# GNN layer with an eight-expert feed-forward layer: all experts for every node, in groups of 256, in place of routing

## What is computed

```python
# gnn
msgs = layernorm(x)[src] * edge_weight[:, None]
agg = segment_sum(msgs, dst, 12500)
x = x + agg @ W.T + b
# feed-forward, E = 8 experts, HID = 1024
xf = layernorm(x)
H = gelu(xf @ W1 + b1)                       # 1024 wide
probs = softmax(H @ Wg + bg)                 # 8 wide
assign = argmax(probs)
for e in range(8):
    y = H @ Wd[e] + bd[e]                    # 1024 x 256 each
    out = out + where(assign == e, probs[:, e:e+1] * y, 0)
x = x + out
```

## Time and profile before

| | |
|---|---|
| median of 3 runs | 2819.68 us (2818.2 to 2826.73) |
| span of the profiled execution | 2820.7 us |
| PE busy | 2418.9 us (86%) |
| POOL busy | 1847.0 us (65%) |
| DVE busy | 988.5 us (35%) |
| ACT busy | 444.4 us (16%) |
| granted TensorE clock, mean | 0.953 |

### The profile page before, as it was taken

One profiled execution on the slowest core, in us unless ns is written; L12 is line 12 of the kernel. 1 busy time (PEld: TensorE's weight loads), 2 busy tenths in 40 slices (PEclk: granted clock), 3 DMA queues, 4 the chain that ended last, 5 costly groups with the idle time before them and its releaser, 6 DMA issues.

```text
span 2820.7 us, 40486 instructions
## 1 busy us (share of the span) xinstructions
PE 2418.9 (86%) x11774; PEld 1410.7 (50%) x11775; DVE 988.5 (35%) x2788; ACT 444.4 (16%) x847; POOL 1847.0 (65%) x1988
## 2 busy tenths in 40 slices
PE   0468998998889889899899899898998968999998
PEld 0133444444444444444444444444444447888887
DVE  8421333333333323333233333233332463333332
ACT  7000011000111000110001101011100102443442
POOL 0677777777777777777777777777777103555553
PEclk9988999999999999999999999999999989999999
DMA  9433444444444444444444444444444254555553
GB/s 390 151 111 112 149 146 137 120 140 149 147 149 125 126 149 148 147 141 120 138 145 148 147 118 132 148 150 148 143 121 133 90 177 129 184 183 176 183 184 126
DMA packets 153599, 420.32 MB, mean 149 GB/s; under 512 B 33320, under 2 KB 67499, under 8 KB 150880
## 3 DMA queue, kind: packets, MB, share of 16 engines
q0 software_dynamic: 100032, 300.27, 35.8%
q1 hardware_dynamic: 53536, 119.73, 11.4%
HBM read 328.02 MB, written 92.82 MB: 149 GB/s over the span
## 4 chain that ended last, share of the span: by engine, by line
POOL 46%; PE 31%; issue 17%; DVE 2%; DMA 2%; DVEq 0%; ACT 0%; SPq 0%; POOLq 0%; ACTq 0%
POOL big L391 46%; PE psA L519 4%; PE psH L560 4%; PE psA L641 3%; PE psG L641 3%; PE psH L641 3%; PE psE L641 3%; PE psR L503 2%; PE psE L509 1%; DMA src_i<-in_srcT 1%; PE psA L581 1%; PE psA L538 1%; PE psH L631 1%; PE psE L631 1%; PE psA L631 1%
## 5 line engine op out<-in xcount | busy, mean ns | idle before, releaser
L391 POOL DMA_INDIRECT big<-xn_table,src_i x1664 | 1615.2, 971 | 581.5 <-issue 580.0
L519 PE MATMUL psA<-w,ident 128*128 128x512 f32 x1664 | 735.5, 595 | 0.0
L519 PEld LDWEIGHTS psA<-w,ident 128*128 128x128 f32 x1664 | 308.5, 190 | 347.9 <-issue 347.9
L503 PE MATMUL psR<-big,sel_narrow 128*32 128x256 f32 x3328 | 258.7, 464 | 220.9 <-DMA big<-xn_table,src_i 158.6
L454 ACT ACTIVATE hidT<-psH,b 128x512 f32<-128x512 f32 x200 | 137.4, 687 | 1651.6 <-PE psH L560 1651.6
L560 PE MATMUL psH<-xn2T,w 128*128 128x512 f32 x800 | 351.4, 592 | 0.7 <-ACT xn2T L449 0.7
L503 PEld LDWEIGHTS psR<-big,sel_narrow 128*32 128x32 f32 x3328 | 116.0, 128 | 369.0 <-issue 333.5
L877 DVE COPY parts<-psR 128x512 f32<-128x512 f32 x104 | 71.8, 690 | 563.3 <-PE psR L503 562.9
L560 PEld LDWEIGHTS psH<-xn2T,w 128*128 128x128 f32 x800 | 152.1, 190 | 181.5 <-issue 179.2
L509 PE MATMUL psE<-w,ident 128*128 128x512 f32 x416 | 224.2, 664 | 0.0
L405 POOL COPY stage<-rel_f 128x1 int32 (+1 forms) x105 | 19.2, 183 | 250.9 <-DVEq L1065 144.3
(11 more groups left out here) (203 smaller groups left out, 2343.4 us busy)
## 6 DMA issues: line engine op xcount, KB each, us to landing
row_table<-rows SPq DMA_DIRECT2D x25, 2064.0 KB, 7.9
big<-xn_table,src_i POOLq DMA_INDIRECT x1664
big<-in_x SPq DMA_DIRECT2D x10, 1280.0 KB, 17.4
xn_table<-big SPq DMA_DIRECT2D x10, 1280.0 KB, 12.8
big<-in_x SPq DMA_DIRECT2D x25, 512.0 KB
row_table<-big SPq DMA_DIRECT2D x25, 512.0 KB, 3.9
big<-in_Wd SPq DMA_DIRECT2D x8, 1024.0 KB, 11.9
hidT<-in_dstT SPq DMA_DIRECT2D x2, 840.0 KB, 30.3
```

Of the source, the lines that this page charges most:

```text
L391: nc.gpsimd.indirect_dma_start(out=xring[:, h * STEP_TILES + j, :], out_offset=None, in_=xn_dram[:, :], in_offset=bass.IndirectOffsetOnAxi ...
L503: mm = nc.tensor.matmul(psQ[j * LANES:(j + 1) * LANES, o * C:(o + 1) * C], sel_narrow[:, t, :], xring[:, t, :], start=(odd == 0), stop=(od ...
L519: nc.tensor.matmul(psA[0][:, :], ident[:, :], w1[:, 0, 0:512], start=True, stop=True)
```

## The change

- Groups are 256 nodes (`GROUP = 256`), so 49 in place of 25. Layer-norm chunks at the start are 7 of 14 rows in place of 10 of 10.
- There is no routing stage and no row table. In a node step PE multiplies the hidden layer of each block of 128 nodes with all of Wd, two experts at a time (512 columns): a `unit` is 8 products, and a group has 2 blocks x 4 pairs = 8 units. DVE adds each unit into x with a factor per node and expert, `mask`, which is the probability for the expert of the largest logit and zero for the others (`route`, `add_unit`). The expert's bias comes from a product of the transposed mask with bd (`bias`).
- A group's first block runs in its own node step, its second block in the next group's node step, mixed with that group's messages, transposes and hidden layer (`group`). The last group's second block comes at the end.
- Wd (8 MB) is loaded once, behind the step tables, and stays in SBUF.
- The products of constants (COVER and FILL) are gone. The first edge products and the placing go by octets of tiles, each octet with its own PSUM bank, copy and semaphore count. The narrow one-hots have one buffer in place of three.
- x is held in two halves by turns, loaded ahead, and stored to the output when all units are added. ACT loads its table for Exp and back for GELU in each group.

```diff
 from contextlib import ExitStack
 import concourse.bass as bass
@@ -30,11 +20,13 @@
 E = 8
 EPS = 1e-5
...
+PAIRS = E // 2
 EDGES = 212500
 STEP_TILES = 16
 NG = -(-EDGES // (P * STEP_TILES))
...
-FILL = 8
 TILES = NG * STEP_TILES
 TABLE = TILES + STEP_TILES
 STEPS = NG + NF
-SLOT = GROUP + P
-NS = 1 << (2 + -(-STEP_TILES * P // GROUP) - 1).bit_length()
+FIELDS = 8
...
+            sp.wait_ge(s_tabs, 1)
             for e in range(E):
-                sp.dma_start(wd[:, e * HC:(e + 1) * HC, :],
-                             Wd[e].rearrange("(c p) o -> p c o", p=P)).then_inc(s_wd, 16)
-            sp.dma_start(bd_bc, bd.rearrange("e c -> (e c)").partition_broadcast(P)).then_inc(s_bd, 16)
+                sp.dma_start(wd[:, :, e * C:(e + 1) * C],
+                             Wd[e].rearrange("(k p) o -> p k o", p=P)).then_inc(s_wd, 16)
...
-            def hidden(f):
+                    nc.scalar.activation(xn2T[:, k, :], psH[k][:, 0:GROUP], ACT.Identity).then_inc(s_xtc, 1)
                 for c in range(HC):
                     act.wait_ge(s_h, f * HC + c + 1)
...
                                          bias=b1[:, c:c + 1]).then_inc(s_gelu, 1)
...
-                routed_act(t, t % RING2)
+                nc.scalar.activation(gate_parts[:, :], psG[:, 0:GROUP], ACT.Identity).then_inc(s_gc, 1)
+                act.wait_ge(s_below, f + 1)
+                nc.scalar.activation(expv[:, :, :], below[:, :, :], ACT.Exp).then_inc(s_exp, 1)
+                nc.scalar.preload_act_table(ACT.Gelu)
+                act.wait_ge(s_mt, f + 1)
+                nc.scalar.activation(mask_t[:, :], psG[0:E, 0:GROUP], ACT.Identity).then_inc(s_mtc, 1)
...
-                                t = h * STEP_TILES + o * OCT + 2 * j + odd
-                                mm = nc.tensor.matmul(psQ[j * LANES:(j + 1) * LANES, o * C:(o + 1) * C],
-                                                      sel_narrow[:, t, :], xring[:, t, :],
+                                t = o * OCT + 2 * j + odd
+                                mm = nc.tensor.matmul(bank[o][j * LANES:(j + 1) * LANES, 0:C], sel_narrow[:, t, :],
+                                                      xring[:, h * STEP_TILES + t, :],
                                                       start=(odd == 0), stop=(odd == 1))
-                    mm.then_inc(s_edge_mm, STEP_TILES)
-                    for _ in range(COVER):
-                        nc.tensor.matmul(psW[:, :], ident[:, :], w1[:, 0, 0:512], start=True, stop=True)
-                    pe.wait_ge(s_parts, g + 1)
+                        mm.then_inc(s_edge_mm, OCT)
                     for o in range(OCTS):
+                        pe.wait_ge(s_parts, g * OCTS + o + 1)
                         for k in range(KC):
-                            at = (o * KC + k) * SPAN
-                            mm = nc.tensor.matmul(psW[:, at:at + SPAN], parts[:, o, k * P:(k + 1) * P],
+                            mm = nc.tensor.matmul(bank[o][:, k * SPAN:(k + 1) * SPAN], parts[:, o, k * P:(k + 1) * P],
                                                   place[:, o, :], start=True, stop=True)
-                    mm.then_inc(s_placed, 1)
-                    for _ in range(FILL):
-                        nc.tensor.matmul(psA[0][:, :], ident[:, :], w1[:, 0, 0:512], start=True, stop=True)
...
+            def dense(to, b, pair, k):
+                return nc.tensor.matmul(to[:, :], hidT[:, k, b * P:(b + 1) * P],
+                                        wd[:, k, pair * 2 * C:(pair + 1) * 2 * C], start=(k == 0), stop=(k == HC - 1))
+            def unit(to, b, pair):
+                for k in range(HC):
+                    mm = dense(to, b, pair, k)
+                mm.then_inc(s_unit, 1)
...
+            def fresh(f, to, k):
+                pe.wait_ge(s_gelu, f * HC + k + 1)
+                mm = dense(to, 0, 0, k)
+                if k == HC - 1:
+                    mm.then_inc(s_unit, 1)
...
-                    mm = nc.tensor.matmul(psG[cg * GATE_COLS:(cg + 1) * GATE_COLS, :], wg[:, c, :], hidT[:, c, :],
-                                          start=(c < 4), stop=(c >= 4))
+                    mm = nc.tensor.matmul(psG[cg * GATE_COLS:(cg + 1) * GATE_COLS, 0:GROUP], wg[:, c, :],
+                                          hidT[:, c, :], start=(c < 4), stop=(c >= 4))
                 mm.then_inc(s_gp, 1)
-                if following is not None:
...
-                        pe.wait_ge(s_ev, f * (2 * QB) + i - 1)
...
+            def first_group():
+                messages(0, psD[1])
+                transpose_xn2(0)
+                pe.wait_ge(s_xtc, KC)
+                pe.wait_ge(s_wd, 16 * E)
+                for c in range(HC):
+                    hidden(0, c)
+                    if c >= 2:
+                        fresh(0, psD[2], c - 2)
+                fresh(0, psD[2], HC - 2)
+                fresh(0, psD[2], HC - 1)
+                gates(0)
+                unit(psD[0], 0, 1)
+                fold_gates(0)
+                unit(psD[1], 0, 2)
+                transpose_mask(0)
+                pe.wait_ge(s_unit_in, 1)
+                unit(psD[2], 0, 3)
+                bias(0)
+            def group(e):
+                f, done = e + 1, e * UNITS
+                pe.wait_ge(s_unit_in, done + 2)
+                unit(psD[0], 1, 0)
+                pe.wait_ge(s_unit_in, done + 3)
+                messages(f, psD[1])
+                pe.wait_ge(s_unit_in, done + 4)
+                unit(psD[2], 1, 1)
+                pe.wait_ge(s_unit_in, done + 5)
+                unit(psD[0], 1, 2)
+                transpose_xn2(f)
+                for k in range(3):
+                    dense(psD[1], 1, 3, k)
+                pe.wait_ge(s_xtc, f * KC + KC)
+                for c in range(HC - 3):
+                    hidden(f, c)
+                    mm = dense(psD[1], 1, 3, c + 3)
+                mm.then_inc(s_unit, 1)
+                pe.wait_ge(s_unit_in, done + 6)
+                for c in range(HC - 3, HC):
+                    hidden(f, c)
+                    fresh(f, psD[2], c - (HC - 3))
+                for k in range(3, HC):
+                    fresh(f, psD[2], k)
+                pe.wait_ge(s_bias_in, f)
+                gates(f)
+                pe.wait_ge(s_unit_in, done + 7)
+                unit(psD[0], 0, 1)
+                fold_gates(f)
+                pe.wait_ge(s_unit_in, done + 8)
+                unit(psD[1], 0, 2)
+                transpose_mask(f)
+                pe.wait_ge(s_unit_in, done + 9)
+                unit(psD[2], 0, 3)
+                bias(f)
+            def last_block():
+                done = (NF - 1) * UNITS
+                for pair in range(PAIRS):
...
+                                         WRAP - 1)
                 with dve.If(wide == 0):
                     def accumulate(o):
                         dve.wait_ge(s_acc, g * STEP_TILES + o * OCT + ACC0)
                         win = agg[:, :, bass.ds(at[o], SPAN)]
-                        nc.vector.tensor_tensor(win, psW[:, o * KC * SPAN:(o + 1) * KC * SPAN]
-                                                .rearrange("p (k n) -> p k n", k=KC),
+                        nc.vector.tensor_tensor(win, bank[o][:, 0:KC * SPAN].rearrange("p (k n) -> p k n", k=KC),
                                                 win, ALU.add).then_inc(s_acc, OCT)
                     nc.vector.tensor_tensor(
                         place[:, :, :], iota[:, 0:SPAN].unsqueeze(1).to_broadcast([P, OCTS, SPAN]),
                         shift_f[:, bass.ds(g * OCTS, OCTS)].unsqueeze(2).to_broadcast([P, OCTS, SPAN]),
...
                         ALU.is_equal)
-                    dve.wait_ge(s_edge_mm, g * STEP_TILES + STEP_TILES + MM0)
-                    nc.vector.tensor_copy(parts[:, :, :], psQ[:, :].rearrange("p (o c) -> p o c", c=C)).then_inc(s_parts, 1)
-                    narrow_onehots(g + 1, start)
-                    dve.wait_ge(s_placed, g + 1)
                     for o in range(OCTS):
+                        dve.wait_ge(s_edge_mm, g * STEP_TILES + (o + 1) * OCT + MM0)
...
+                    narrow_onehots(g + 1)
+                    for o in range(OCTS):
+                        dve.wait_ge(s_placed, g * OCTS + o + 1)
                         accumulate(o)
-                    narrow_weights(g + 1, start)
+                    narrow_weights(g + 1)
...
+                dve.wait_ge(s_g, f + 1)
                 dve.sem_inc(s_pass_dve, 1)
-                for i in range(2 * QB):
...
+                link(nc.vector.tensor_tensor(
+                    lg[:, :, :], psG[:, fold_at:fold_at + QB * E].rearrange("p (q e) -> p q e", e=E),
+                    bg_bc[:, :].unsqueeze(1).to_broadcast([P, QB, E]), ALU.add))
+                link(nc.vector.tensor_reduce(best[:, :], lg[:, :, :], AX.X, ALU.max))
+                nc.vector.tensor_tensor(below[:, :, :], lg[:, :, :], best[:, :].unsqueeze(2).to_broadcast([P, QB, E]),
```

(85 more changed lines are left out.)

631 lines of the change are left out of this document (181 added, 450 removed).

## The result

The changed kernel takes 4457.3 us (median of 4 runs, 4455.2 to 4459.6) against 2820.6 us: ratio 1.581, 95% interval 1.578 to 1.583. The forecast was 4239 us, slower; the range ended at 4460. The profiled execution has a span of 4456.7 us.

A forecast was written before the change was run, and what follows sets the result against it. PE's dense work was taken to bound the kernel: 149 us until the first group, 12 for its uncovered start, 3280 for groups, 649 for edge steps, 144 for the clock and 5 at the end gave 4239 us; range 4060 to 4460.

The forecast's parts named there:

- The dense products decide: In each group, 64 dense products of 0.864 us are 55.3 of PE's 66.9 us; 49 groups take 3280 us.
- Rival (d): Dense products: much cheaper than the old row, 0.41 us each, so not slower, 2820 us; chance 0.02.
- No holes inside a group: Inside a group, PE runs without waits; normalization, route chain and table loads lie under the units and cost nothing.
- Rival (a): Inside groups, route chain or normalization comes late and PE waits, 5 us per group: 4484 us; chance 0.12.
- Edge steps: Between groups, DVE's loop paces: 101 steps of 5.95 us plus 1.0 us for each of 48 stretches, 649 us.
- a cycle of not about 6 us: Edge stretches: the forecast is wrong if a stretch's cycle is not about 6 us.
- PE's own work plus about 2 us of its loop: Edge steps, lower bound: PE's work plus about 2 us of loop, from a 1.74 us gap, 4.9 us a step.
- The upper end of 7 us a step: Edge steps, upper bound: 7 us a step if the hand-offs by octet are slower.
- The clock: Around each stretch's end, PE's clock falls for want of constant products: 3 us for each of 48 stretches, 144 us.
- Rival (b): In each group, the clock stays low far in, 8 us lost instead of 3: 4479 us; chance 0.07.
- Rival (c): Edge steps as cheap as PE allows, 4.9 us, and the clock never falls: 3989 us; chance 0.07.
- Start and end: First group starts at 149 us and costs 12 more uncovered; Wd's loads cost up to 10; the end 5.

The follow-up runs named there:

- e4: Changed kernel with the dense products over only 4 of the 8 hidden slices: 3131.2 us.
- e8: Changed kernel with the experts' products on bfloat16 operands, gates and choice of expert still float32: 2795.3 us, ratio 0.992 to the kernel before.
- e2: Changed kernel without the never-taken wide branch and the load of its flag, on PE alone: 4390.2 us.
- e3: Changed kernel without the never-taken wide branch and the load of its flag, on DVE alone: 4446.1 us.
- e11: Changed kernel with eight products of constants behind the placing of every edge step: 4717.7 us, ratio 1.673 to the kernel before.
- e1: Changed kernel with four products of constants behind the placing of every edge step: 4366.4 us, ratio 1.546 to the kernel before.
- e9: Changed kernel with bfloat16 experts' products and without the wide branch on PE and DVE: 2776.5 us, ratio 0.984 to the kernel before.
- e10: Changed kernel with bfloat16 experts' products, no wide branch on PE and DVE, three products of constants behind the placing: 2749.5 us, ratio 0.975 to the kernel before.
- e12: Old, routed kernel with the routed tiles' expert product on bfloat16 operands: 2727.6 us, ratio 0.964 to the kernel before.
- e5: Old kernel without its products of constants (COVER and FILL at 0): 2811.3 us, ratio 0.9973 to the kernel before.
- e7: Changed kernel with the octets' split undone, one bank, one count and one DVE copy of 512 columns: 4484.5 us.

## Why the prediction was right in direction and 218 us short

- **The dense products decide.** Right, and shown twice. A group's PE work was 66.9 us as summed; halving the products (e4) took 1326 us off, making them four times cheaper (e8) took 1662 us off. POOL's gathers left the path. Rival (d) is out.
- **No holes inside a group.** Right. The normalization, the route chain and the table loads stayed under the units; the only waits, 4.7 us for the sums (L412), 6.7 us for the normalized rows (L420) and 0.5 us for ACT (L428), are the first group's. Rival (a) is out. It comes true only when the units shrink, as e8 shows.
- **Edge steps.** This is the term that failed, and the forecast's own sign of being wrong, a cycle of not about 6 us, came up. "What paces two steps in a row is now DVE, in a loop" was wrong, and so was "PE's own work plus about 2 us of its loop": behind the placing PE idles 2.9 us on average, and its turn takes 3.5 to 4.4 us from its last wait. The 1.74 us before 1263.97 in the earlier trace rows is not the turn. The rows ahead of it in the kernel before show why:

```profile
1259.26 1.25 PE L581 MATMUL psA<-ident,hidT 128*128 128x128 f32 x8 [0.19 <-DVE rows L943]
1260.35 0.96 PE L587 MATMUL psE<-fold,big 128*128 128x8 f32 x8
1261.16 1.07 PE L547 MATMUL psH<-ident,big 128*128 128x128 f32 x8
```

The last wait seen there ends at 1259.26. Folds and transposes still ran while the sequencer went round, and the next step's products came 4.71 us after that wait; 1.74 us is what stuck out. e2 against e3 shows that PE's loop is what ends last (67 against 11 us), e11 that the hole is filled by four products and not by more. The upper end of 7 us a step was too low as well.
- **Where the 217 us are.** Two thirds, 142 us, are the first steps: forecast 6.95 us with the start behind the group, measured 9.91. DVE's loop behind the bias took 3.86 us, not 2.5, so the placing began 5.6 us in, and behind it came PE's bare turn, for whose idle part the forecast had 1.5 to 2 us. The later steps, without the clock, took 6.27 us for 5.95. That this is near is luck: a wrong pacer with nearly the right time.
- **The clock.** Mechanism right, size small: 3 us a stretch were forecast, the table above gives 4.2, and the busy time that e1 gave back (108 us in dense products, 88 in L374) 4.1. Rival (b), 8 us lost in the group, is out (2.4 us). Rival (c), steps as cheap as PE allows, fell with the edge-step term.
- **The range.** 4457 lies 3 us under its upper end. The range was drawn for halves of (a), (b) and (c), and none of them is what made the miss; that it still holds the result is luck too.
- **Start and end.** The first group ended at 203.75, where the terms give 200; the end took 3.8 us for 5. Wd was no wait.

The rule that the forecast took from the Trainium skill, "TensorE: Matmul & The Clock Gate", section "Loop structure matters more than you think", held in every stretch: the later steps' first products took 3.25 to 3.64 us where the first step's took 1.93, and the group's first unit 8.6 to 10.2 where others took 7.03. The same page's 131 ns, section "Back-to-back issue gap", did not hold: a float32 record of 512 columns stayed at 0.43 us, and the bfloat16 product at 0.226.

Did routing pay? With the float32 product yes, by 1.5 times. With the cheap product all experts beat the old float32 kernel by 2.5% at best, but the routed kernel with the same product is about 1% faster still (2727.6 against 2749.5 us, ratios 0.964 against 0.975), and it had nothing like the shorter loops of e9 and e10. Not tested are larger groups, which would have fewer first steps, and a second buffer for the narrow one-hots.

## What to carry to other kernels

Price the added products first, number times a measured duration of the same shape and type; here eight times the products for one expert's result lost to routing even when a product had become 3.8 times cheaper (e10 against e12), and then the waits that the long products had covered were the bill. When an engine's filler or long work is taken away, its own loop (branches, loads of fields) comes out from under it: measure the turn from the last wait ahead of it to the next product, not by the idle gap, which work still queued makes shorter. In these kernels fillers paid only where PE was the bound (e1 against e5), only as many as the hole took (e11), and not in the first steps, behind another wait that had already let the clock fall.

## What the runs showed of the hardware beyond that

- With nothing queued behind the placing, TensorE's sequencer needed 3.5 to 4.4 us from its last wait in a step round the loop (the rest of the tests, loop end, two field loads, tests, the flag) to the next product; e3, e4 and e7 give the same range. Without the flag load and the wide branch (e2) it was 2.7 to 3.8. How the rest divides among tests and loads isn't shown. At a group's end, where the last unit and the bias were queued, the same way round cost nothing: L374 begins at 2138.11, right behind the bias.
- DVE's weights and PE's next products: where DVE was the last (10 cases in e7), the product started 0.06 us after the weights' end. In the changed kernel the gap is 0.7 to 2.5 us at all edge steps that start behind another step, so DVE's weights were not what they waited for.
- 128x128 by 128x512: 0.864 us in float32, 0.226 us in bfloat16 (16 in 3.62 us), 3.8 times.
- At a mean granted clock of 0.72 over 2085 us (e5) the old kernel lost nothing.
